# Statistics of x moved from VectorE to ScalarE in a fused cross-attention and routed-FFN kernel, with several waits and banks moved

## What is computed

```
x = x + cross_attention(layernorm(x), ctx)     # 16 heads of 16, all in fp32, softmax over all keys
x = x + expert_mlp(layernorm(x))               # one of 32 experts for each token, by argmax of router logits
```

## Time and profile before

| | us |
|---|---|
| median of 3 runs (lowest, highest) | 1183.46 (1182.79, 1188.08) |
| profiled execution, its own time | 1188.65 |
| span in the profile | 1186.8 |
| PE busy | 1090.2 (92%) |
| DVE busy | 946.0 (80%) |
| POOL busy | 875.5 (74%) |
| ACT busy | 799.1 (67%) |
| granted PE clock, mean | 0.975 |

### The profile page before, as it was taken

One profiled execution on the slowest core, in us unless ns is written; L12 is line 12 of the kernel. 1 busy time (PEld: TensorE's weight loads), 2 busy tenths in 40 slices (PEclk: granted clock), 3 DMA queues, 4 the chain that ended last, 5 costly groups with the idle time before them and its releaser, 6 DMA issues. The chain is left out here.

```text
span 1186.8 us, 38807 instructions
## 1 busy us (share of the span) xinstructions
PE 1090.2 (92%) x15164; PEld 817.5 (69%) x15164; DVE 946.0 (80%) x2360; ACT 799.1 (67%) x1860; POOL 875.5 (74%) x1709
## 2 busy tenths in 40 slices
PE   5999999999999999999999999999998539999992
PEld 4676777777777777777777777777776339888772
DVE  5688888888888888888888888888888538777672
ACT  4777777777777777777777777777775326566551
POOL 5467777777777777777777777777776547777776
PEclk9999999999999999999999999999999759999997
DMA  6516222522222222222222222222210146666650
GB/s 217 167 55 144 77 79 83 149 79 77 84 77 73 74 73 79 77 74 74 73 75 81 81 75 74 73 77 81 68 41 34 58 155 202 205 209 205 203 160 12
DMA packets 91282, 120.37 MB, mean 101 GB/s; under 512 B 14096, under 2 KB 74139, under 8 KB 90909
## 3 DMA queue, kind: packets, MB, share of 16 engines
q1 hardware_dynamic: 77278, 84.04, 25.7%
q0 software_dynamic: 13824, 33.85, 7.8%
HBM read 60.61 MB, written 59.31 MB: 101 GB/s over the span
## 5 line engine op out<-in xcount | busy, mean ns | idle before, releaser
L575 DVE TENSOR_REDUCE mx<-m 128x4 bf16<-128x512 f32 x512 | 323.7, 672 | 3.3 <-PE m L790 3.2
L462 ACT ACTIVATE arena<-sc 128x512 f32<-128x512 f32 x512 | 264.6, 603 | 47.1 <-PE sc L814 46.9
L424 POOL DMA_INDIRECT out<-arena x160 | 157.3, 983 | 61.2 <-issue 35.4
L396 POOL DMA_INDIRECT pages<-row,slot_i x128 | 129.7, 1014 | 57.1 <-issue 53.8
L805 PE MATMUL sc<-qk 32*128 32x256 f32 x2048 | 166.6, 396 | 0.7 <-DVE bo_s L680 0.5
L823 PE MATMUL pB<-arena 128*32 128x128 f32 x4096 | 158.6, 277 | 0.6 <-DVE row L584 0.6
L831 PE MATMUL pB<-wo_s,aT 128*128 128x288 f32 x512 | 149.5, 415 | 6.9 <-DVE aT L606 6.9
L823 PEld LDWEIGHTS pB<-arena 128*32 128x32 f32 x4096 | 99.1, 110 | 43.9 <-issue 42.4
L773 PE MATMUL pA<-cHi,wqkv 128*128 128x512 f32 x252 | 119.6, 476 | 9.5 <-DVE wqkv L648 9.5
L773 PE MATMUL pA<-xnT,wqkv 128*128 128x512 f32 x372 | 126.2, 447 | 0.0
L595 DVE STREAM_TRANSPOSE tr<-pB 128x512 f32<-128x512 f32 x128 | 91.5, 714 | 36.8 <-PE pB L823 35.1
(11 more groups left out here) (158 smaller groups left out, 2489.4 us busy)
## 6 DMA issues: line engine op xcount, KB each, us to landing
arena<-pages SPq DMA_DIRECT2D x160, 130.0 KB, 2.5
cT<-ctxT SPq DMA_DIRECT2D x64, 256.0 KB, 3.5
xs<-x_in SPq DMA_DIRECT2D x128, 128.0 KB, 2.2
pages<-empty SPq DMA_DIRECT2D x120, 130.0 KB
pages<-empty SPq DMA_DIRECT2D x1, 5200.0 KB, 19.9
out<-arena POOLq DMA_INDIRECT x160
w2s<-w SPq DMA_DIRECT2D x1, 2080.0 KB
qk<-w SPq DMA_DIRECT2D x1, 2064.0 KB, 8.5
```

The lines of the kernel that those rows point to most:

```text
L396: pool.indirect_dma_start(pages, bass.IndirectOffsetOnAxis(slot_i[:, u:u + 1], 0), row[:, q % 4, u, 0:ROW], None, bounds_check=last_slot, ...
L424: pool.indirect_dma_start(out_rows, bass.IndirectOffsetOnAxis(pr[:, r, COL_TOKEN:COL_TOKEN + 1].bitcast(U32), 0), pr[:, r, X0:X0 + D], Non ...
L462: act.activation(pt[:, u % 2, g].rearrange("p i k -> p (i k)"), sc[g][:, :], ACT.Exp).then_inc(S["exp_out"], 1)
L575: ins = dve.tensor_reduce(mx[:, 32 * g:32 * g + 4], mb[i][:, :].rearrange("p (h k) -> p h k", h=4), AX.X, ALU.max)
```

## The change

Five things are changed at once.

1. `stats1` goes from DVE to ACT. In place of `bn_stats` and `bn_aggr`, ACT makes two passes over each batch of `x`, a Copy and a Square, each with an accumulated sum. They stand behind `squares` and ahead of `proj_copy` in every block, for group s+3, and in the set-up for groups 0, 1 and 2.
2. `rstd1` on POOL takes sums now (seven small operations, five before), and stands at the head of POOL's step, ahead of the scatter and of `rstd2`.
3. `best` on DVE stands ahead of `residual` in block 1. The slot sum writes integers directly, into two buffers, so POOL's `slots_as_integers` is gone; `meta` has two operations instead of five.
4. `logits_transpose` and `ranks` on PE use bank `sc[0]`, not `sc[3]`. They no longer wait for the fourth exponential of the block. `project` is cut 3+3, 4+2, 4+2, 3+3 matmuls over blocks 0 to 3, where it was 3+3 in each.
5. The reciprocals `inv` lie in a free piece of the PSUM bank `pB`, not in SBUF.

```diff
@@ gpsimd
             def rstd1(q):
-                after(pool, "agg1_out", 4, q, 3)
+                after(pool, "stat1_out", 4, q, 3)
...
-                pool.tensor_scalar(v, g[:, :, 1], EPS, None, ALU.add).then_inc(S["var1_out"], 1)
+                pool.tensor_scalar(sx1[:, q % 2, :], sx1[:, q % 2, :], -1.0 / D, None, ALU.mult).then_inc(S["mean1_out"], 1)
+                pool.tensor_scalar(sq1[:, q % 2, :], sq1[:, q % 2, :], EPS, None, ALU.add).then_inc(S["eps1_out"], 1)
+                after(pool, "mean1_out", 1, q, 0)
+                pool.tensor_tensor(mm1[:, :], sx1[:, q % 2, :], sx1[:, q % 2, :], ALU.mult).then_inc(S["mm1_out"], 1)
...
+                pool.tensor_tensor(v, sq1[:, q % 2, :], mm1[:, :], ALU.subtract).then_inc(S["var1_out"], 1)
...
             for s in range(-1, NQ + 2):
+                if live(s + 2):
+                    rstd1(s + 2)
                 if live(s - 2):
-                    slots_as_integers(s - 2)
                     scatter(s - 2)
                 if live(s - 1):
                     rstd2(s - 1)
                     scale_logits(s - 1)
-                if live(s + 2):
-                    rstd1(s + 2)
@@ scalar
+            def stats1(q, u):
+                act.wait_ge(S[f"ld_x{q % 4}_{u}"], q // 4 * 16 + 16)
+                if q >= 2:
+                    after(act, "rstd1_out", 1, q - 2, 0)
+                if q * QB + u >= 1:
+                    act.wait_ge(S["stat1_out"], q * QB + u)
+                act.activation(junk_x[:, 0], xs[:, q % 4, u, 0:D], ACT.Copy, accum_out=sx1[:, q % 2, u:u + 1]).then_inc(S["sumx_out"], 1)
+                act.activation(junk_x[:, 1], xs[:, q % 4, u, 0:D], ACT.Square, scale=D ** -0.5,
+                               accum_out=sq1[:, q % 2, u:u + 1]).then_inc(S["stat1_out"], 1)
             act.wait_ge(S["ld_wk"], 16)
             act.activation(wqkv[:, 1, 0], wraw[:, 1], ACT.Copy).then_inc(S["wk_hi"], 1)
+            for u in range(QB):
+                stats1(0, u)
...
+            for u in range(QB):
+                stats1(1, u)
             act.wait_ge(S["ld_b"], 80)
...
                     if live(q1):
                         squares(q1, u1)
+                    if s >= 0 and live(s + 3):
+                        stats1(s + 3, u)
                     if live(q):
...
                         proj_copy(q, n)
@@ vector
                     if u == 1 and s >= 0 and live(s + 1):
                         x_logits(s + 1)
+                    if u == 1 and live(s - 1):
+                        best(s - 1)
                     if live(q1):
                         residual(q1, u1)
...
-                    if u == 1 and live(s - 1):
-                        best(s - 1)
-                    if u == 2 and live(s + 3):
-                        stats1(s + 3, (2, 3))
@@ tensor
-                        project(pq, n, (0, 1) if s < 0 else (0,))
+                        project(pq, n, 0, 6 if s < 0 else (3, 4, 4, 3)[u])
...
                     if u == 1 and s >= 0 and live(s + 1):
-                        after(pe, "exp_out", 16, s, 4 * u + 3)
                         logits_transpose(s + 1)
                     if u == 2 and live(s - 1):
                         if live(s):
-                            after(pe, "exp_out", 16, s, 4 * u + 3)
+                            after(pe, "exp_out", 16, s, 4 * u)
                         ranks(s - 1)
...
-                        project(pq, n, (1,))
+                        project(pq, n, (3, 4, 4, 3)[u], 6)
```

More of the change, by code:

```diff
@@ L120, in build @@
         t1 = sb("t1", [QB, E])
-        slot, slot_i = sb("slot", [QB]), sb("slot_i", [QB], U32)
-        tok, expert = sb("tok", [QB]), sb("expert", [QB])
+        slot_i = sb("slot_i", [2, QB], U32)
         empty = sb("empty", [ROW])
@@ L141, in build @@
         pA, pB = ps("pA"), ps("pB")
+        inv = pB[:, 480:496]
         names = """ld_c0 ld_c1 ld_cst ld_wk ld_wq ld_wv ld_b ld_wo ld_wr ld_w1 ld_w2 fill fill0 fill1 fill2 fill3
@@ L332, in meta @@
                     pool.wait_ge(S["ld_cst"], 16)
-                    pool.tensor_copy(tok[:, :], cst[:, C_TOKEN:C_TOKEN + QB]).then_inc(S["tok_out"], 1)
+                pool.tensor_scalar(row[:, q % 4, :, COL_TOKEN].bitcast(I32), cst[:, C_TOKEN:C_TOKEN + QB], float(q * QB * P), None, ALU.add)
                 after(pool, "idx_out", 1, q, 0)
[L335 to L340, removed]
+                pool.tensor_scalar(row[:, q % 4, :, COL_EXPERT].bitcast(I32), idx[:, :], -1.0, float(E), ALU.mult, ALU.add).then_inc(S["meta_out"], 1)
             def each(t):
@@ L487, in rank_copy @@
                     after(act, "own_slots", 1, q - 1, 0)
-                act.activation(rks[:, :], sc[3][:, 0:(QB + 1) * E], ACT.Copy).then_inc(S["rk_out"], 1)
+                act.activation(rks[:, :], sc[0][:, 0:(QB + 1) * E], ACT.Copy).then_inc(S["rk_out"], 1)
             def mxT_copy(q, u):
@@ L529, in _ @@
                             norm1(1, v)
+                        stats1(2, u)
             def pnT_copy(n):
@@ L557, in own @@
                 dve.wait_ge(S[name], value)
[L559 to L568, removed]
-                    dve.bn_aggr(ag1[:, q % 2, u, :], st1[:, u, :]).then_inc(S["agg1_out"], 1)
             def maxima(q, u, half_):
@@ L598, in normalise @@
                 after(dve, "tr_out", 4, q, u)
-                dve.reciprocal(inv[:, :], tr[:, :].rearrange("p (k r) -> p k r", r=32)[:, :, HD]).then_inc(S["inv_out"], 1)
+                dve.reciprocal(inv, tr[:, :].rearrange("p (k r) -> p k r", r=32)[:, :, HD]).then_inc(S["inv_out"], 1)
                 after(dve, "inv_out", 4, q, u)
@@ L642, in slot_sum @@
                 if q >= 1:
-                    after(dve, "slot_int", 1, q - 1, 0)
-                dve.tensor_reduce(slot[:, :], t1[:, :, :], AX.X, ALU.add).then_inc(S["slot_out"], 1)
+                    after(dve, "scattered", 64, q - 1, 63)
+                dve.tensor_reduce(slot_i[:, q % 2, :], t1[:, :, :], AX.X, ALU.max).then_inc(S["slot_out"], 1)
             def low(w):
@@ L702, in _ @@
                         scan(s - 1)
-                    if u < 2 and live(s + 3):
-                        stats1(s + 3, (u,))
                     if live(q1):
@@ L765, in transposes, with project @@
                 ins.then_inc(S["xnT_done"], 1)
-            def project(q, n, halves=(0, 1)):
+            def project(q, n, first, last):
                 c = n % 2
                 w = 1 if n < 2 else 0
-                for i in halves:
-                    for a, b in HI_LO:
-                        src = (cHi, cLo)[b][:, q % 2] if n < 2 else xnT[:, b]
-                        ins = pe.matmul(proj_bank(q, n)[:, :], wqkv[:, w, a, i, c * P:(c + 1) * P], src[:, i, :],
-                                        start=(i == 0 and (a, b) == HI_LO[0]), stop=(i == 1 and (a, b) == HI_LO[-1]))
-                if halves[-1] == 1:
+                for k in range(first, last):
+                    i, (a, b) = k // 3, HI_LO[k % 3]
+                    src = (cHi, cLo)[b][:, q % 2] if n < 2 else xnT[:, b]
+                    ins = pe.matmul(proj_bank(q, n)[:, :], wqkv[:, w, a, i, c * P:(c + 1) * P], src[:, i, :],
+                                    start=(k == 0), stop=(k == 5))
+                if last == 6:
                     ins.then_inc(S["proj_done"], 1)
```

51 lines of the change are left out of this document (23 added, 28 removed).

## The result

The changed kernel takes 1232.06 us (median of 4 runs, 1228.54 to 1234.14). The kernel before, run beside it, takes 1185.77 us (4 runs, 1182.79 to 1189.86). The ratio is 1.0385, with a 95% interval of 1.0341 to 1.0429: slower by 46 us, where 1228 was forecast. The profiled execution has a span of 1232.0 us, against 1186.8 before.

A forecast was written before the change was run, and what follows sets the result against it. PE was taken as the bound, held each block by ACT's `mxT` copy. Terms 37.8 (27 steps, some 1.4 us each) + 1 - 0.7 + 5 = 43.1 us raised the median 1183.46 to 1226.6; 1.5 for the clock gave 1228, range 1204 to 1246.

The forecast's parts named there:

- The pair costs 0.82 us: On ACT, the two passes over one batch take 0.82 us with accumulator reads hidden, 3.3 us of each step.
- Rival 2: On ACT, a pair of passes costs only 0.61 us by the skill's figure, giving 1211 us; chance 0.06.
- The slack of 0.48 us before the `mxT` copies: ACT's idle time of 0.48 us in block 3, 0.47 in block 0; lateness counted as 0.34 and 0.30 us.
- Block 1, `z_out` at 529.4 and DVE waiting 0.55 us: Moved `rstd1` delays POOL's `z_out`, holding `best`, the residual and the next `mxT` copy: 0.85 us more per step.
- Block 2 at -0.08: To the copy at 510.93: slack 0.53 us and 0.27 from PE's ranks against 0.82, so 0.08 us less.
- Steps 0 and 1 at +1, steps 29 to 31 at -0.7: First steps have no late `z_out`, +1 us; last steps have no statistics, only PE's gains, -0.7 us.
- The clock at +1.5: Allowance of 1.5 us over the whole kernel for a fall of PE's clock here and there.
- Rival 3: PE's clock falls in many steps, in block 2: 1248 us if in half of them, 1268 in all; chance 0.13.
- The waits taken from PE, at nothing: Removed PE waits for exponentials (31.4 us for values, 8.4 for ranks) counted at nothing except 0.27 us in block 2.
- The set-up at +5: `norm1` of group 0 stands behind group 1's pairs, starting at 16.2 to 16.6 us: +5 us, bounds 4 and 7.
- Rival 1: `z_out` is in time, so DVE doesn't wait 0.55 us in 27 steps: 15 us less, 1213 us; chance 0.16.
- rival 4: Faster: pairs fit into ACT's idle time and PE keeps the gain of the removed waits, 1168 us; chance 0.07.

The follow-up runs named there:

- experiment 1: The changed kernel with the statistics back on DVE, all else as changed: 1160.57 us, ratio 0.975 to the kernel before.
- experiment 3: The changed kernel with the two ACT passes moved ahead of `squares` in each block: 1166.18 us, ratio 0.9807 to the kernel before.
- experiment 4: The changed kernel with `best` behind the residual again on DVE in block 1: 1192.93 us, ratio 1.0043 to the kernel before.
- experiment 7: The changed kernel with both ACT passes reading one column of x instead of 256: 1177.29 us, ratio 0.991 to the kernel before.
- experiment 2: The kernel before with only the ACT passes and `rstd1`'s new operations put in; PE, DVE and POOL keep their order: 1238.41 us, ratio 1.0415.
- experiment 6: The kernel before with PE's part of the change alone (waits moved, projections split 3, 4, 4, 3, ranks and logits in `sc[0]`): 1178.84 us, ratio 0.9938.
- experiment 10: The changed kernel with statistics back on DVE and without PE's part, leaving the orders of POOL and DVE: 1173.65 us, ratio 0.9881 to the kernel before.
- experiment 11: The changed kernel with twelve added unused matmuls on PE ahead of `subtract_max` in block 2: 1216.84 us, ratio 1.0245 to the kernel before.

## Why the prediction held, step by step

The time, 1232 for 1228, is right. The mechanism of the main term is shown by experiments 1, 3, 4 and 7. But the plain step was priced 13 us too high, the clock and the late issues 16 us too low, and the sum hid it: that the total came within 4 us is in part luck. One of the prediction's own signs of being wrong, a low granted clock in the middle of the kernel, did come, in 7 of the 27 steps.

- **The pair costs 0.82 us**: 0.80. That the accumulator read hides is only half true: the second pass starts 0.31 us after the first has been started plus 0.09 us for the read (532.03, 532.34, 532.43). The Trainium skill ("ScalarE: Activation LUTs", What ACT_TABLE_LOAD costs) gives 186 ns + 0.833 ns an element and 93 ns of overlap; the trace agrees for the activation itself (401 ns measured, 399 by the page, and 0.31 us to the next instruction). Rival 2's 0.61 us a pair has two such steps and leaves out the read behind each pass.
- **The slack of 0.48 us before the `mxT` copies**: it was about 0.57. The idle time in the earlier trace rows ends where the copy starts, but without a wait the copy starts 0.1 us before the instruction ahead of it ends (534.16, where that one ends at 534.26). Block 3 lost 0.20 us by the copies' starts, not 0.34. Block 0 lost 0.29 (0.30 predicted).
- **Block 1, `z_out` at 529.4 and DVE waiting 0.55 us**: the chain holds. `rstd1` took 2.60 us as estimated, and DVE waits 0.46 us. But the term was 0.37 us in a plain step, not 0.85. POOL's chain from `rstd1` to `z_out` took 11.5 us and not the 12.1 that the prediction's terms add up to (the pause before the first indirect DMA is 0.38 us, before it was 0.78; `rstd2`'s last operation 0.21, before 0.47). `best` took 1.02 us and not 1.12, and blocks 3 and 0 brought less lateness along. The prediction's own times also give 533.54 for the copy, 1.41 us late, so 0.77 and not 0.85: 2 us in 27 steps. Experiment 4 shows that the place of `best` decides.
- **Block 2 at -0.08**: 0.01. Together 0.87 by the copies' starts (0.92 by the whole steps, against the mean before) where 1.4 was predicted: 25 us in 27 steps, not 37.8.
- **Steps 0 and 1 at +1, steps 29 to 31 at -0.7**: 0, and -1.7 with the pages behind them.
- **The clock at +1.5**: 9.9 us by the steps. This is the step that failed. Rival 3 came in a quarter of the steps, and the argument against it, that the two idle stretches lie apart, was wrong: they need not lie together, as 441.00 to 444.50 shows. One fall cost 1.42 us (1.7 at most had been priced).
- **The waits taken from PE, at nothing**: nearly. The whole of the change but the passes gives 4 to 6 us in experiment 2 against the changed kernel, no more than the noise. It was right that they are worth more where ACT isn't late (8 and 13 us in experiments 6 and 10).
- **DVE's reduction hides**: yes; its busy time in steps 2 to 28 is 620.5 us, where it was 669.7, and the steps are longer all the same. (`meta` has two operations where there were four, 508.06 to 508.48 us before, so POOL loses two by it, not three.)
- **The set-up at +5**: +4.0. `norm1` started at 15.82, where 16.2 to 16.6 was predicted. PE's clock was not low there, and that was luck: in experiment 3, with the same instructions in the set-up, it fell twice and the first scores started at 39.5 us, +6.0.
- **Not foreseen**: the late issues of an indirect DMA, 7.8 us, and all seven falls came in steps that had one. They counted only because `best` stood ahead of the residual (experiment 4). Why an issue takes 1.49 us in some steps and not in others stays open.

Rival 1 (`z_out` in time) is excluded by DVE's wait of 0.46 us, rival 4 by the missing idle time before the copies. What rival 4 needed, passes in ACT's idle time, is what experiment 3 does, and it came to 1166, beside 1168. Why the clock falls in just seven of the fifteen steps with a late issue was not settled.

## What to carry to other kernels

An engine that is idle for 30% of the time can be full at the one place that counts: look for the wait that holds the bound engine, and count the slack right before its releaser. Work that has its data long before belongs ahead of an instruction that waits, not behind it; two statements swapped were worth 66 us here. Where a change makes PE stand idle twice within some microseconds, price a fall of its clock from a row where it did fall, and don't count on a distance between the two. When an experiment gains what was expected, look in its trace for what else went: in experiment 11 the late issues did, and the gain can't be put down to the edit alone.

## What the runs showed of the hardware that was not expected

- An accumulator read on ACT is 188 ns long, and holds the next activation back by 0.09 us (experiment 7: four instructions over one column follow each other every 0.09 us).
- Where a pair waits for the one before it to be complete, it costs 1.0 us: in the set-up the passes over the four blocks start at 6.37, 7.36, 8.36 and 9.36 us.
- `normalise`'s product (128x256), with one operand moved from SBUF to PSUM, takes 421 ns (107 times, 100 to 900 us), 509 before. The Trainium skill ("SBUF — State Buffer", SBUF: two separate sides) says that a VectorE operation with two SBUF inputs shares a port with GpSimd; the two means agree with that, and no run here isolates it.
- The clock went to 1.2 GHz in 7 of 15 places where PE had been busy some 1.8 of 3.50 us (1.87 before 444.50 us), though its two waits there were 0.56 and 0.96 us and no longer. It stayed at 2.4 GHz in 12 places with 2.3 or 2.4 of 3.50. One fall cost 1.42 us.
- An indirect DMA of the scatter takes 0.98 us to issue (the first of four 1.13), and in fourteen of 27 steps one of the four takes 1.49.
